# Three layers on one core: constant products on TensorE in the routing stages, slot loads ahead of the linear layer's setup, and the last layer's roots in two calls

## What is computed

```python
x = x + attn_a(layernorm(x))     # 16 heads of 64, causal softmax, x is [1, 2048, 128]
x = x + ffn(layernorm(x))        # 8 experts, each token goes to one
x = x + attn_b(layernorm(x))     # linear attention, 16 heads of 8
x = x + ffn(layernorm(x))        # the same 8 experts, same weights

def ffn(h):                      # h: [2048, 128]
    logits = (h @ w_red) @ normalised(wg).T
    gates = softmax(logits)
    idx, score = argmax(gates), gates[argmax]
    y = gelu(h @ w1[idx] + b1[idx]) @ w2[idx] + b2[idx]      # hidden size 512
    return y * score
```

## Time and profile before

| | us |
|---|---|
| timed runs | 1242.02, 1244.05, 1243.08; median 1243.08 |
| the profiled execution | 1235.74 |
| its span, first to last instruction | 1234.0 |
| TensorE busy | 1135.5 (92%) |
| VectorE, GpSimd, ScalarE busy | 930.9, 832.8, 808.1 |
| mean granted TensorE clock | 0.963 |

### The profile page before, as it was taken

One profiled execution on the slowest core, in us unless ns is written; L12 is line 12 of the kernel. 1 busy time (PEld: TensorE's weight loads), 2 busy tenths in 40 slices (PEclk: granted clock), 3 DMA queues, 4 the chain that ended last, 5 costly groups with the idle time before them and its releaser, 6 DMA issues. The chain is left out here.

```text
span 1234.0 us, 24704 instructions
## 1 busy us (share of the span) xinstructions
PE 1135.5 (92%) x8010; PEld 847.9 (69%) x8010; DVE 930.9 (75%) x2054; ACT 808.1 (65%) x2248; POOL 832.8 (67%) x814
## 2 busy tenths in 40 slices
PE   6999999999999999999999999999999669687477
PEld 4776677677767776777677767767776559354377
DVE  5887878787787778778877787788787546598645
ACT  6877676767786767777777767776777346342355
POOL 3687678857786788677677757785878435585434
PEclk9999999999999999999999999999999879799579
DMA  5000810081018002700450063002004232100131
GB/s 145 27 1 1 210 49 2 6 229 35 1 35 224 2 1 58 209 1 2 117 141 1 2 176 92 1 18 52 2 1 126 86 92 67 35 1 1 56 98 50
DMA packets 72908, 75.71 MB, mean 61 GB/s; under 512 B 8487, under 2 KB 61869, under 8 KB 72784
## 3 DMA queue, kind: packets, MB, share of 16 engines
q1 hardware_dynamic: 69776, 67.80, 20.6%
q0 software_dynamic: 3008, 6.34, 1.5%
HBM read 15.34 MB, written 42.91 MB: 47 GB/s over the span
## 5 line engine op out<-in xcount | busy, mean ns | idle before, releaser
L604 DVE TENSOR_REDUCE at_nmax<-at_ps 128x1 f32<-128x512 f32 (+3 forms) x640 | 374.6, 603 | 122.0 <-PE at_ps L853 119.1
L510 POOL TENSOR_SCALAR at_prob<-at_prob,at_scale 128x512 f32<-128x512 f32 (+3 forms) x307 | 424.5, 1401 | 2.0
L850 PE MATMUL at_ps<-at_k_st,at_q_parts 128*128 128x512 f32 (+3 forms) x640 | 285.6, 446 | 4.0 <-DVE at_q_parts L663 2.0
L721 ACT ACTIVATE at_prob<-at_ps,at_nmax 128x512 f32<-128x512 f32 (+3 forms) x416 | 259.9, 631 | 43.5 <-DVE at_nmax L604 42.7
L879 PE MATMUL at_ps<-at_probT,at_v 128*64 128x256 f32 (+1 forms) x2304 | 270.1, 374 | 0.6 <-DVE at_probT L627 0.6
L734 ACT ACTIVATE at_probT<-at_ps 128x512 f32<-128x512 f32 (+1 forms) x288 | 165.2, 574 | 148.8 <-PE at_ps L864 122.6
L853 PE MATMUL at_ps<-at_k_st,at_q_parts 128*128 128x512 f32 (+3 forms) x640 | 252.2, 394 | 0.0
L627 DVE COPY at_probT<-at_ps 128x512 f32<-128x512 f32 (+1 forms) x288 | 189.1, 657 | 51.6 <-PE at_ps L864 42.8
L510 POOL TENSOR_SCALAR late<-late,at_scale 128x512 f32<-128x512 f32 (+1 forms) x168 | 226.4, 1364 | 1.6
L864 PE MATMUL at_ps<-ident,at_prob 128*128 128x128 f32 x1440 | 220.1, 273 | 5.1 <-DVE at_probT L627 4.3
L879 PEld LDWEIGHTS at_ps<-at_probT,at_v 128*64 128x64 f32 x2304 | 152.1, 136 | 102.5 <-issue 40.9
(11 more groups left out here) (241 smaller groups left out, 1488.3 us busy)
## 6 DMA issues: line engine op xcount, KB each, us to landing
slots_in<-empty SPq DMA_DIRECT2D x6, 2967.0 KB, 18.9
slots_in<-empty SPq DMA_DIRECT2D x6, 2838.0 KB, 18.4
at_q_parts<-at_q_parts SPq DMA_DIRECT2D x64, 256.0 KB, 3.5
f_xs<-slots_in SPq DMA_DIRECT2D x46, 129.0 KB
late<-in_L_ffn_w_dram SPq DMA_DIRECT2D x1, 2048.0 KB, 9.0
late<-in_L_ffn_w_dram SPq DMA_DIRECT2D x4, 512.0 KB, 6.6
rows<-in_L_attn_a_x_dram SPq DMA_DIRECT2D x4, 256.0 KB, 3.8
rows<-new_x SPq DMA_DIRECT2D x4, 256.0 KB, 3.7
```

The lines of the kernel that those rows point to most:

```text
L510: pool.tensor_scalar(cols, cols, scale[:, k, u, c:c + 1], None, ALU.mult).then_inc(s_fix["pool"], 1)
L604: dve.tensor_reduce(nmax[:, q % 2, 2 * i + h, c:c + 1], bank, AX.X, ALU.max, negate=True).then_inc(s_max, 1)
L721: act.activation(prob[ROW_HOME[j]][u][:, c * BANK:c * BANK + w], ring[use_of["score", p, j, i, h, c] % RING][:, 0:w], ACT.Exp, bias=nmax[: ...
L850: pe.matmul(bank[:, 0:w], q_hi[h][:, r * P:(r + 1) * P], keys, start=True, stop=False)
```

## The change

Six loops of bf16 products of the two constant matrices (128 x 128 by 128 x 128) are added on TensorE, with results that nobody reads: 240 at the end of attention; in f0, 60 before the slots and 100 after them; 50 at the start of linear attention; in f1, 40 at the start and 170 between the routing and the slots, behind a wait for `s_slot`. The work beside f0 moves into the slots: the four DMAs between loads 7 and 8, VectorE's part into round 12, TensorE's to `xT` of slot 14, ScalarE's to `xT` of slot 16; the bank is now 6, and TensorE's wait for the copy moves to linear attention, where it already stood. In the routing of f1 the roots are taken for tiles 0 to 3 and then for tiles 4 to 15 at once, all statistics stand before the first choice, and each chunk is transposed, scored and ranked in turn.

```diff
@@ attention, tensor, after the planner's list
+                for _ in range(240):
+                    pe.matmul(turn_ps[0][:, 0:P], keep["all"][:, :], keep["before"][:, :], start=True, stop=True)
@@ ffn, sync
-                if beside:
-                    beside["sync"](sp)
                 sp.wait_ge(keep["s_slot"] if scattered else s_slot, 2)
                 sp.wait_ge(keep["s_scattered"] if scattered else s_scat, 16 * NT)
                 for s in range(SLOTS):
                     k = s % LOADED
+                    if beside and s == LOADED:
+                        beside["sync"](sp)
@@ ffn, vector
                 def norm(c):
                     rows = slice(TPC * c, TPC * (c + 1))
-                    dve.wait_ge(s_std, c + 1)
-                    dve.reciprocal(rstd[:, rows], rstd[:, rows]).then_inc(s_rstd, 1)
-                    dve.wait_ge(s_rstd, c + 1)
+                    if c < 2:
+
+                        dve.wait_ge(s_std, c + 1)
+                        rows = slice(TPC, NT) if c else rows
+                        dve.reciprocal(rstd[:, rows], rstd[:, rows]).then_inc(s_rstd, 1)
+                        dve.wait_ge(s_rstd, c + 1)
...
                 if not scattered:
                     statistics(0)
-                    statistics(1)
                     norm(0)
                     for c in range(1, NC):
+                        statistics(c)
+                    choose(0)
+                    for c in range(1, NC):
                         norm(c)
-                        if c + 1 < NC:
-                            statistics(c + 1)
-                        if c >= 2:
-                            find_place(c - 2)
-                        choose(c - 1)
-                    find_place(NC - 2)
-                    choose(NC - 1)
+                        find_place(c - 1)
+                        choose(c)
                     find_place(NC - 1)
...
-                if beside:
-                    beside["vector"](dve)
...
+                    if beside and (stage, s) == ("weights", LOADED + U):
+                        beside["vector"](dve)
@@ ffn, scalar
                 if not scattered:
+                    for rows in (slice(0, TPC), slice(TPC, NT)):
+                        act.wait_ge(s_aggr, rows.stop)
+                        act.activation(rstd[:, rows], mv[:, rows, 1], ACT.Sqrt, bias=keep["eps"][:, 0:1]).then_inc(s_std, 1)
                     for c in range(NC):
-                        if c == NC - 1:
-                            exponential(0)
-                        act.wait_ge(s_aggr, (c + 1) * TPC)
-                        rows = slice(c * TPC, (c + 1) * TPC)
-                        act.activation(rstd[:, rows], mv[:, rows, 1], ACT.Sqrt, bias=keep["eps"][:, 0:1]).then_inc(s_std, 1)
-                        if c:
-                            act.wait_ge(s_xnTp, c)
-                            act.activation(xnT[:, (c - 1) * BANK:c * BANK], ps[(c - 1) % 2][:, :], ACT.Copy).then_inc(s_xnT, 1)
...
+                        act.wait_ge(s_xnTp, c + 1)
+                        act.activation(xnT[:, c * BANK:(c + 1) * BANK], ps[c % 2][:, :], ACT.Copy).then_inc(s_xnT, 1)
                         exponential(c)
-                if beside:
-                    beside["scalar"](act, ps[4])
...
+                    if beside and (stage, s) == ("xT", LOADED + 2 * U):
+                        beside["scalar"](act, ps[6])
@@ ffn, tensor
                 if not scattered:
-                    turn(0)
-                    for c in range(1, NC):
+                    for _ in range(40):
+                        pe.matmul(ps[5][:, 0:P], keep["all"][:, :], keep["before"][:, :], start=True, stop=True)
+                    for c in range(NC):
                         turn(c)
-                        score_experts(c - 1)
-                        rank(c - 1)
-                    score_experts(NC - 1)
-                    rank(NC - 1)
-                if beside:
-                    pe.wait_ge(beside["tensor"](pe, ps[4]), 1)
+                        score_experts(c)
+                        rank(c)
+
+
+                if not scattered:
+                    pe.wait_ge(s_slot, 2)
+                for _ in range(60 if scattered else 170):
+                    pe.matmul(ps[6][:, 0:P], keep["all"][:, :], keep["before"][:, :], start=True, stop=True)
...
+                    if beside and (stage, s) == ("xT", LOADED + U + 2):
+                        beside["tensor"](pe, ps[6])
...
                 in_turn({"xT": 1, "h": 2, "y": 3}, emit)
+                if scattered:
+
+                    for _ in range(100):
+                        pe.matmul(ps[7][:, 0:P], keep["all"][:, :], keep["before"][:, :], start=True, stop=True)
@@ linear_attention, tensor
                 pe.wait_ge(li["s_const"], 2)
                 pe.wait_ge(li["s_wT"], 1)
+                for _ in range(50):
+                    pe.matmul(out, keep["all"][:, :], keep["before"][:, :], start=True, stop=True)
```

More of the change, by code:

```diff
@@ L1142, in _ @@
                 if not scattered:
+                    for rows in (slice(0, TPC), slice(TPC, NT)):
+                        act.wait_ge(s_aggr, rows.stop)
+                        act.activation(rstd[:, rows], mv[:, rows, 1], ACT.Sqrt, bias=keep["eps"][:, 0:1]).then_inc(s_std, 1)
                     for c in range(NC):
-                        if c == NC - 1:
-                            exponential(0)
-                        act.wait_ge(s_aggr, (c + 1) * TPC)
-                        rows = slice(c * TPC, (c + 1) * TPC)
-                        act.activation(rstd[:, rows], mv[:, rows, 1], ACT.Sqrt, bias=keep["eps"][:, 0:1]).then_inc(s_std, 1)
-                        if c:
-                            act.wait_ge(s_xnTp, c)
-                            act.activation(xnT[:, (c - 1) * BANK:c * BANK], ps[(c - 1) % 2][:, :], ACT.Copy).then_inc(s_xnT, 1)
-                    act.wait_ge(s_xnTp, NC)
-                    act.activation(xnT[:, (NC - 1) * BANK:NC * BANK], ps[(NC - 1) % 2][:, :], ACT.Copy).then_inc(s_xnT, 1)
-                    for c in range(1, NC):
+                        act.wait_ge(s_xnTp, c + 1)
+                        act.activation(xnT[:, c * BANK:(c + 1) * BANK], ps[c % 2][:, :], ACT.Copy).then_inc(s_xnT, 1)
                         exponential(c)
-                if beside:
-                    beside["scalar"](act, ps[4])
                 def emit(stage, s, k):
+                    if beside and (stage, s) == ("xT", LOADED + 2 * U):
+                        beside["scalar"](act, ps[6])
                     if stage == "xT":
@@ L1307, in on_tensor @@
         last.then_inc(s_wTp, 1)
-        return s_wT
     def on_scalar(act, bank):
```

## The result

The change takes 1248.93 us (median of 6 executions, 1245.83 to 1249.84), the kernel before 1243.53 us (6 executions, 1242.02 to 1244.24): ratio 1.0043, 95% interval 1.0033 to 1.0054. It is slower by 5.4 us, where 5.5 were forecast, and 1248.93 us stand against the 1248.6 forecast. The profiled execution of the change took 1248.83 us. First its page: the span, and the granted clock in 40 slices.

A forecast was written before the change was run, and what follows sets the result against it. TensorE mostly waits in three half-clock stretches, where the clock costs only what lies on the path. 5.7 - 3.5 + 0.45 - 0.4 + 3.3 = +5.5 us on 1243.08 gave 1248.6 us, range 1240 to 1254.

The forecast's parts named there:

- The price: All added products on TensorE: one 128-column bf16 product takes 57 ns at full clock, 110 ns at half.
- rival (a): All added products: dearer, about 80 ns each, so +16.3 us in all, 1259.4 us; chance 0.10.
- Part 1: End of attention: the 240 products end at 998.1 and f0 begins at 999.0 instead of 993.28, +5.7 us.
- Part 2: Start of f0: loads first and full clock, -3.5 us; the folding moved into the slots, +0.45 us.
- Part 3: Linear attention: 50 products hidden under a wait, less time at half clock, -0.4 us, bounds 0 and -0.7.
- Part 4: Routing of f1: the 170 products stand before the first slot and end after its data land, +3.3 us.
- rival (b): Routing of f1: the 40 products raise the clock and it holds; sum +1.3 us, 1244.4 us; chance 0.17.
- (c): All added products: free, the 240 averaging under 41 ns; sum -4.5 us, 1238.6 us; chance 0.13.
- (d): All added products: they don't raise the clock and cost 110 ns each; above 1265 us; chance 0.02.
- The base: Whole kernel: profiled 1235.74 us plus 5.5 gives 1241.3; the timed median's 7.3 us excess is added unchanged.

The follow-up runs named there:

- before_again: The kernel before, unchanged, profiled a second time: 1243.60 us, ratio 1.0001 to the kernel before.
- no170: The change without the 170 products before f1's slots and their wait for the slots' table: 1246.00 us, ratio 1.0021 to the kernel before.
- none: The change without any of the constant products, the moved code kept: 1241.94 us, ratio 0.9996 to the kernel before.
- no_small: The change without its groups of 60, 100, 50 and 40 products, the 240 and 170 kept: 1250.43 us, ratio 1.0069 to the kernel before.
- p120: The change with 120 products in place of 240 at the end of attention: 1245.11 us, ratio 1.0014 to the kernel before.
- run 23: Not the name of a run: the words belong to "had run 23 products", a count of products that one stream finished before its first pause.

## Why the prediction was right, point by point

**The price held.** 57 ns were taken; 60 took 3.51 us, 100 took 5.75, 50 took 2.95: 57 to 59 ns. At half clock the 40 took 4.43 us, 111 ns, where 110 were taken. The Trainium skill's 81 ns ("TensorE: Matmul & The Clock Gate", section "Back-to-back issue gap") is not what these streams show, and rival (a) falls. Over the 240 as a whole, with part at half clock and pauses with no releaser in the trace, it was 18.5 us / 240 = 77 ns.

**Part 1** was +5.7. The block came 19.68 - 13.56 = 6.1 us later behind the last rank product than in before_again, but 19.68 - 10.83 = 8.9 us later than in the trace that the forecast started from. Two errors that cancelled, which is luck: the products took 18.5 us where 15.6 were forecast, since the clock rose only at 991.5, after 8.6 us and not 4 (nor within the 2 to 7 that the range allowed for); and the kernel before itself needs 13.56 - 10.83 = 2.7 us more there than its first trace showed, because of the late signal.

**Part 2** was -3.5, and +0.45 in the slots. From the block's start to gelu's table 8.90 us (before_again) became 5.55, so -3.35, and the slots from table to last product went from 43.74 to 44.18, +0.44. By its two runs the moved work is worth 1.5 to 1.9 us of the net. The rest is the clock that the 240 and the 60 bring together: the table comes after 5.55 and 5.70 us in the two traces with both (after, no170), and after 6.5 to 7.0 in every other trace with the moved work, with the 60 alone, the 240 alone, the 120 and the 60, or none.

**Part 3** was -0.4. Column c is 89.53 to 90.16 in the seven kernels with the 50 products and 88.14 to 90.17 in the seven without: no gain shown, and none of the short ones has them. Its bound of 0 was the better value: with the 50 the clock is up at first, falls 6.2 to 9.3 us after the layer's start and is not back for good before 13.0 us. The products put the low stretch a little later, they don't remove it.

**Part 4** was +3.3; column d rose by 46.07 - 42.60 = 3.5 against before_again, and by 5.2 against the first trace, where the late signals of the routing are missing: luck again. The order of routing costs 1.8 us by its own run; the forecast hid it under the products. The 40 do raise the clock: it rises 2.7 to 5.6 us after f1's start in the four traces with them, and not before the 170 or the slots in the ten others. What that buys is not settled: in the change the first scores took 0.8 us less, but d is even between no170 and none. The 170 took 11.12 us (11.6 were forecast) and cost 1.6 in d (after against no170) to 3.4 (no_small against none), 2.9 by the medians. p120 has the same code in f1 as the change, and its d is 1.2 us longer, its 170 taking 12.30 us: single traces are that coarse. What the 170 give back is the clock inside f1's slots: e is 51.2 to 51.3 in all four traces with them. But so it is in six of the ten without, so the gain is up to 2.3 us in some executions and nothing in others. The routing stayed at half but for 3.5 us, so rival (b) falls; (c) and (d) fall with the pace and the clock.

**The base** was the weak step. "I add the same difference there" took the 7.3 us between the profiled execution and the median as even over both kernels, and worked out every part from an execution in which the clock rose early in linear attention and the late signals were missing. By that trace the change's profiled execution should have taken 1241.3 us; it took 1248.83. Before_again is longer than the first trace by 4.1 us up to f0's start, 2.0 in linear attention and 1.7 in f1's routing. The sum held because the change pays these delays too, so that they drop out of the difference; the forecast had not seen them. Against before_again, span for span, the change is 1247.1 - 1241.8 = +5.3: 6.1 - 2.9 - 0.5 + 3.5 + 0.0 from columns a to e, and -0.9 because its attention happened to end earlier (982.91 against 983.80).

## What to carry to other kernels

Work that only keeps TensorE's clock up takes time itself, and here it never paid: of the eight kernels with such products none was faster than before. The 240 and 60 together did keep the clock through f0's start, which bought 1 us there (b is 57.50 against 58.55 in none), and put the block off by 6 us. Either group alone bought nothing. Taking setup loads and weight folding out from in front of the first loads gave 1.5 to 1.9 us in two runs; it is the only part of the change worth keeping. And a trace is one draw: look whether its own time lies among the timed ones, and take a second of the same kernel, before tenths are read from it.

## What was not expected of the hardware

A signal of TensorE can come late: between the start of the last rank product at attention's end and VectorE's copy that waits for it there were 0.2 us in one trace and 3.5 to 4.0 us in thirteen, with products behind it or without. In f1's routing ScalarE waited in the same way (1173.28, "3.91 <-remote"). In the five traces with products behind the rank products, these pause for 0.4 to 1.0 us after 23 to 25 of them, with no releaser in the trace, and each time the copy starts 0.08 to 0.09 us after they go on (987.00 and 987.09 in p120, 986.82 and 986.91 in the change). So the late signal and TensorE's pause end together. Their cause stays open; no run removed either.

The rise of the clock is not a fixed time after work begins. These are the rows with the rise at attention's end in p120 and in the change:

```profile
985.00:986.00 1.00, 0.95 (x9) 0.65 (x7) 0.00 (x0) 0.00 (x0) 0.52 (x1) 0.61 0.19 66
...
990.00:992.00 2.00, 2.00 (x25) 2.00 (x24) 0.17 (x1) 0.00 (x0) 1.39 (x3) 0.62 0.22 81
```

It came 2.5 us after the first product in p120 and 8.6 us after it in the change, for the same code up to there; the one stream had run 23 products before its first pause, the other 19. By the table above this spread, and not the edits, sets 2 us of linear attention and 2 us of f1's slots in single executions, and 2 us of f0 between the two traces of the moved work alone. Why it rises early in one execution and late in another, no run shows.
